# An expert network's first layer as 20 block products in place of 22, with the next group's first four products ahead of the token tiles

## The chip, the cores and the metric

One core of a Trainium2 chip. The metric is the device time of one launch in microseconds; three runs of the kernel before are shown, and one execution under the profiler.

## What is computed

Two blocks of a graph network with a feed-forward part, on 1250 nodes ("tokens") of 512 features. The change lies in the last part, the eight experts that every token passes, mixed by the leaf probabilities of a small decision tree:

```python
b, s, dim = x.shape                              # 1250 tokens, 512 features
leaf_probs = _leaf_probs(flat_x, rw, rb)         # [tokens, 8]
h = jnp.einsum('nd,edh->neh', flat_x, w1) + b1[None]     # first layer: 512 -> 2048 for each of 8 experts
h = jax.nn.gelu(h, approximate=False)
y = jnp.einsum('neh,ehd->ned', h, w2) + b2[None]         # second layer: 2048 -> 512
out = jnp.einsum('ned,ne->nd', y, leaf_probs)
```

The result is added to the running rows of the tokens. All else (the graph sums, the routing of the other expert layer) is left as it was.

## The kernel before

The changed part is `phase_tree`. The 8 x 2048 hidden columns are worked through in 64 **groups** of 256; two groups make a **pair** (the code's quarter `Q`), the first with even number `G`, the second with odd. Matrices in fp32 are multiplied in three passes (`cut_products`, lines 528 to 530): a rounded high part of each operand and the rest, high x high, high x low, low x high. So every operand has a "hi" (a ScalarE copy into the rounded type) and a "lo" (a VectorE subtraction).

First layer of a group: a 256 x 512 block of weights times 512 x 1250 tokens. The tokens stand in three blocks of 416, 416 and 418. The two of 416 are worked by Strassen's scheme, seven products of half blocks, of two 128-row slices each; the third directly, in eight slices. That is 7 x 2 + 8 = 22 block products of 128 x 128 x (416 or 418), 66 matmuls. The sums of weight blocks that Strassen's scheme wants are made by GpSimd (`weight_sums`, lines 1741 to 1746, four sums of 256 columns), their hi by ScalarE (L1785), their lo by VectorE (L2064). The sums of token blocks are made once, at the start (L1769, L2144, L2167 and around). Products are mixed by VectorE out of PSUM (L2079 to L2101, five a group); gelu with the bias on ScalarE, then hi (L1852) and lo (L2105).

Second layer of a pair: ten tiles of 125 tokens, each four slices of hidden columns x three passes, 120 matmuls of 512 columns (`second`); VectorE adds a tile into the token rows, weighted by the leaf probability (L2132). Eight tiles end in the pair itself, tiles 8 and 9 (`LATE`) inside the next pair's first group.

Every engine has its own queue, written out by hand as a loop over the groups, and works it strictly in order; engines wait for each other by counting semaphores. TensorE's queue holds in each group some products of the first layer, then "slots" with work of the second layer, then the rest. PSUM has eight banks: four for the token tiles, four for the first layer. Weights come by DMA from SyncE's queue into one buffer of 256 x 512 (`raw1`), from which GpSimd, ScalarE and VectorE read. The buffers of the weight sums are double, and the plain sums lie in the same place as their low parts.

Names of rows: `x_sums_hi`, `x_block_hi` are token operands, `w_sums`, `w_hi`, `w_lo` weights, `hidden` the gelu's in- and output.

Of the kernel before, what the change touches and what calls it, by code (L numbers as in the profile page):

```python
# [55 lines left out]
TBLOCKS = [(0, 416), (416, 832), (832, 1250)]  # L56
TBW = 416
# [1486 lines left out]
STEPS = 48  # L1544


def tree_buffers(nc, g, low, middle, high):
    room = Room(nc, low)
    g.xchi = room("x_sums_hi", [128, 7, 2, TBW], F32R)
    sums_at = room.next  # L1550
    g.xclo = room("x_sums_lo", [128, 7, 2, TBW], F32R)
    g.xcsum = Room(nc, sums_at)("x_sums", [128, 7, 2, TBW], F32)
    xf_at = room.next
    g.xf = room("f_xT", [128, KD, N], F32)
    node_at = room.next
    g.node_z = room("node_z", [7, N], F32)
    g.low_end = room.next
# [3 lines left out]
    g.b2b = Room(nc, node_at)("b2_by_token", [128, 2, D], F32)  # L1561
    assert over.next <= node_at and node_at + 2 * D * 4 <= g.low_end

    room = Room(nc, middle)
    g.p1 = room("first_product", [128, TBW], F32)
    g.u2 = room("second_sum", [128, TBW], F32)
    g.u3 = room("third_sum", [128, TBW], F32)
# [4 lines left out]
    g.x2hi = room("x_block2_hi", [128, KD, BW], F32R)  # L1572
    g.x2lo = room("x_block2_lo", [128, KD, BW], F32R)
    s1hi = room("w1_sums_hi1", [128, 4, 2, 128], F32R)
    sums_at = room.next
    s1lo = room("w1_sums_lo1", [128, 4, 2, 128], F32R)
    s1 = Room(nc, sums_at)("w1_sums1", [128, 4, 2, 128], F32)
# [5 lines left out]
    g.w1hi = room("w1_hi", [128, 2, KD, 256], F32R)  # L1583
    g.w1lo = room("w1_lo", [128, 2, KD, 256], F32R)
    s0hi = room("w1_sums_hi0", [128, 4, 2, 128], F32R)
    sums_at = room.next
    s0lo = room("w1_sums_lo0", [128, 4, 2, 128], F32R)
    s0 = Room(nc, sums_at)("w1_sums0", [128, 4, 2, 128], F32)
    g.shi, g.slo, g.ssum = (s0hi, s1hi), (s0lo, s1lo), (s0, s1)
    g.branch = room("branch", [TR, NT, 2, 7], F32)  # L1590
    g.pairs = room("branch_pairs", [TR, NT, 4], F32)
    g.leaf = room("leaf_by_token", [TR, NT, NE], F32)

# [5 lines left out]

def phase_tree(nc, sem, g, produce, rows):  # L1600
# [4 lines left out]
    w1hi, w1lo, w2hi, w2lo, raw1, raw2 = g.w1hi, g.w1lo, g.w2hi, g.w2lo, g.raw1, g.raw2  # L1605
# [6 lines left out]
    moved = sem("f_moved")  # L1612
    x_sum = sem("f_x_sum")
    x_sum_pool = sem("f_x_sum_pool")
# [9 lines left out]
    w1_hi = sem("t_w1hi")  # L1624
    w1_lo = sem("t_w1lo")
    s_sum = sem("t_s_sum")
    s_hi = sem("t_s_hi")
    s_lo = sem("t_s_lo")
# [3 lines left out]
    p1_moved = sem("t_p1_moved")  # L1632
# [12 lines left out]
    P1, P5, P6, P2, P7, P4, P3, D0, D1 = range(1, 10)  # L1645
    U2, U3, C22, C21, C12 = range(1, 6)
    ACTIVE_AT = {(0, 0): 1, (1, 1): 2, (0, 1): 3, (1, 0): 4, (2, 0): 5, (2, 1): 6}
    BANK_A, BANK_F, BANK_E, BANK_B = 4, 5, 6, 7
    X11, X21, X22, T1, T2, T3, T4 = range(7)
# [7 lines left out]
    def made(G, which):  # L1657
        return 9 * G + which

    def summed(G, which):  # L1660
        return 5 * G + which
# [5 lines left out]
    def block_count(Q, b, m):  # L1667

        return 6 * (2 * Q + m // 2) + ACTIVE_AT[b, m % 2]

    def tokens(of, b, m):
        return of[:, m, TBLOCKS[b][0]:TBLOCKS[b][1]]

# [7 lines left out]
    def wait_block_free(eng, Q, b):  # L1681
        if Q:
            eng.wait_ge(used, y_count(Q - 1, last_tile(b)))
# [8 lines left out]
    def x_block(i, j):  # L1692

        return g.xf[:, 2 * i:2 * i + 2, TBLOCKS[j][0]:TBLOCKS[j][1]]

    with nc.Block() as block:
        @block.sync
        def _(sp):
            def load1(n):
                e, p = divmod(n, 8)  # L1700
                if n:
                    sp.wait_ge(w1_lo, n)
                    sp.wait_ge(s_sum, 4 * n)
                sp.dma_start(raw1[:, :, :], w1_d[e, :, :, p * 256:(p + 1) * 256]).then_inc(w1_in, 16)
# [10 lines left out]
            for G in range(GROUPS):  # L1715
                if G + 2 < GROUPS:
                    load1(G + 2)
                if G + 1 < GROUPS:
                    load2(G + 1)
                if G % 8 == 0:  # L1720
                    e = G // 8
                    if e == 0:
                        sp.wait_ge(node_turned, 1)
                    elif e >= 2:
                        sp.wait_ge(b2_added, NT * (e - 1))
                    sp.dma_start(g.b2b[:, e % 2, :], g.b2[e:e + 1, :].partition_broadcast(128)).then_inc(b2_in, 16)
            for i in [0, 1, 2, 3, 4, 5, 7, 9]:
                store_out(sp, i)
# [3 lines left out]
        def _(q):  # L1732
            def weight_sums(n):

                a11, a12 = raw1[:, 0:2, 0:128], raw1[:, 2:4, 0:128]
                a21, a22 = raw1[:, 0:2, 128:256], raw1[:, 2:4, 128:256]
                s1, s2, s3, s4 = (g.ssum[n % 2][:, i] for i in range(4))
# [4 lines left out]
                q.tensor_tensor(s3, a11, a21, ALU.subtract).then_inc(s_sum, 1)  # L1742
                q.wait_ge(s_sum, 4 * n + 1)
                q.tensor_tensor(s2, s1, a11, ALU.subtract).then_inc(s_sum, 1)
                q.wait_ge(s_sum, 4 * n + 3)
                q.tensor_tensor(s4, a12, s2, ALU.subtract).then_inc(s_sum, 1)

            weight_sums(0)
            q.wait_ge(moved, 7)
            q.tensor_tensor(g.xcsum[:, T3], x_block(1, 1), x_block(0, 1),  # L1750
                            ALU.subtract).then_inc(x_sum_pool, 1)
# [15 lines left out]
        def _(a):  # L1767
            def hi_sum(which):
                a.activation(g.xchi[:, which], g.xcsum[:, which], ACT.Copy).then_inc(x_hi, 1)  # L1769

            def w1_high(n):
# [626 lines left out]
```

## Time and profile before

| | us |
|---|---|
| median of three runs | 2363.72 (2363.37 to 2366.75) |
| profiled execution | 2362.39, its span 2360.6 |
| TensorE busy in the span | 2232.0 (95%) |
| VectorE, ScalarE, GpSimd busy | 1358.8, 919.0, 408.6 |

The expert stretch begins near 650 us and lasts to the end. A row of the timeline has its start, its duration, engine, line, operation, what is written and read, and in brackets how long the engine stood idle before and who released it. Matmuls overlap in the rows, since their ends include the run through the array; pace is read from start to start. PEclk is the granted TensorE clock as a share of 2.4 GHz.

### The profile page before, as it was taken

Reading aid. Unit: us, or ns where it says so; the run is one execution under the profiler, and the core shown is the slowest. Engines: PE = TensorE matmul, PEld = TensorE weight load, DVE = VectorE, ACT = ScalarE, POOL = GpSimd, SP = SyncE. Lnnn points to the kernel's source line nnn. Section 1 sums busy time; section 2 is a strip of 40 time slices with the busy share of each in tenths; the row PEclk is TensorE's granted clock in tenths of the full one; section 3 lists DMA queues with packets and bytes.
Section 4 is the critical chain, followed back from the end, with each engine's and each line's share of the span. In section 5 each row is a group of like instructions: output and inputs, shape, how many; then the busy total and the mean of one; then the engine's idle time right before and its main releaser. Section 6 shows DMA issues by size and latency. Waiting matters only on the chain.

```text
span 2360.6 us, 31808 instructions
## 1 busy us (share of the span) xinstructions
PE 2232.0 (95%) x12255; PEld 1978.7 (84%) x12255; DVE 1358.8 (58%) x2143; ACT 919.0 (39%) x1474; POOL 408.6 (17%) x378
## 2 busy tenths in 40 slices
PE   3998998579999999999999999999999999999999
PEld 3887996449678888888888888888888888888887
DVE  7995356645465555555555555555555555555554
ACT  1335335245354344343334444443333443433332
POOL 1553000110121121121111121121111121121110
PEclk9999998689999999999999999999999999999999
DMA  2000202250011111111111111111111111111111
GB/s 69 2 2 1 72 1 81 83 162 14 27 41 36 45 43 43 45 44 42 36 37 42 44 45 42 43 45 36 36 41 45 36 50 45 36 45 41 36 36 53
DMA packets 70689, 101.92 MB, mean 43 GB/s; under 512 B 5519, under 2 KB 40927, under 8 KB 70543
## 3 DMA queue, kind: packets, MB, share of 16 engines
q1 hardware_dynamic: 67243, 94.20, 12.2%
q0 software_dynamic: 3040, 5.19, 0.8%
q8 instruction: 100, 1.64, 0.3%
q10 hardware_dynamic: 260, 0.51, 0.1%
q14 instruction: 46, 0.38, 0.1%
HBM read 92.14 MB, written 7.74 MB: 42 GB/s over the span
## 4 chain that ended last, share of the span: by engine, by line
PE 73%; DVE 1%; ACT 1%; issue 0%; DVEq 0%
PE psum L528 24%; PE psum L529 24%; PE psum L530 24%; DVE x_sums_lo L2144 0%; PE psum L1902 0%; ACT f_rows L522 0%; DVE stats L486 0%; DVE x_rows L2154 0%; PE psum L1892 0%; DVE norm_shift L495 0%; ACT x_sums_hi L1806 0%; PE psum L1909 0%; ACT L1836 0%; ACT dev L517 0%; DVE x_sums L2167 0%
## 5 line engine op out<-in xcount | busy, mean ns | idle before, releaser
L529 PE MATMUL psum<-w_lo,hidden_hi 128*125 128x512 f32 x1280 | 506.2, 395 | 0.0
L528 PE MATMUL psum<-w_hi,hidden_hi 128*125 128x512 f32 x1280 | 505.1, 395 | 0.0
L530 PE MATMUL psum<-w_hi,hidden_lo 128*125 128x512 f32 x1280 | 504.7, 394 | 0.0
L2132 DVE SCALAR_TENSOR_TENSOR x_rows<-psum,leaf_by_token,x_rows 125x512 f32<-125x512 f32 x320 | 232.5, 747 | 301.2 <-PE psum L530 301.2
L2105 DVE TENSOR_TENSOR hidden_lo<-hidden,hidden_hi 128x416 fp32r<-128x416 f32 (+1 forms) x384 | 258.9, 674 | 198.3 <-ACT hidden_hi L1852 198.2
L1741 POOL TENSOR_TENSOR w_sums<-w_raw 128x256 f32<-128x256 f32 x64 | 48.8, 762 | 1407.9 <-PE psum L530 1329.5
L530 PEld LDWEIGHTS psum<-w_hi,hidden_lo 128*125 128x125 f32 x1280 | 237.4, 185 | 60.7
L528 PEld LDWEIGHTS psum<-w_hi,hidden_hi 128*125 128x125 f32 x1280 | 237.9, 186 | 53.7
L529 PEld LDWEIGHTS psum<-w_lo,hidden_hi 128*125 128x125 f32 x1280 | 237.0, 185 | 53.0
L1841 ACT ACTIVATE hidden<-hidden,b1cols 128x416 f32<-128x416 f32 x192 | 122.8, 640 | 310.8 <-DVE hidden L2089 253.6
L1830 ACT ACTIVATE first_product<-psum 128x416 f32<-128x416 f32 x64 | 33.3, 520 | 516.5 <-PE psum L530 516.5
L1852 ACT ACTIVATE hidden_hi<-hidden 128x416 fp32r<-128x416 f32 (+1 forms) x384 | 212.5, 553 | 12.2
L528 PE MATMUL psum<-x_sums_hi,w_sums_hi 128*128 128x416 f32 x512 | 180.9, 353 | 1.1 <-DVE hidden L2089 1.1
L528 PE MATMUL psum<-x_block_hi,w_hi 128*128 128x418 f32 x512 | 180.6, 353 | 0.0
L530 PE MATMUL psum<-x_sums_hi,w_sums_lo 128*128 128x416 f32 x512 | 180.5, 353 | 0.0
L529 PE MATMUL psum<-x_block_lo,w_hi 128*128 128x418 f32 x512 | 180.1, 352 | 0.0
L529 PE MATMUL psum<-x_sums_lo,w_sums_hi 128*128 128x416 f32 x512 | 179.9, 351 | 0.0
L530 PE MATMUL psum<-x_block_hi,w_lo 128*128 128x418 f32 x512 | 179.5, 351 | 0.0
L528 PE MATMUL psum<-x_sums_hi,w_hi 128*128 128x416 f32 x384 | 135.5, 353 | 0.0
L529 PE MATMUL psum<-x_sums_lo,w_hi 128*128 128x416 f32 x384 | 135.1, 352 | 0.0
L530 PE MATMUL psum<-x_sums_hi,w_lo 128*128 128x416 f32 x384 | 135.1, 352 | 0.0
L2079 DVE TENSOR_TENSOR second_sum<-psum,first_product 128x416 f32<-128x416 f32 x64 | 37.8, 591 | 136.5 <-PE psum L530 136.5
(335 smaller groups left out, 3955.2 us busy)
## 6 DMA issues: line engine op xcount, KB each, us to landing
w_raw<-in_w SPq DMA_DIRECT2D x128, 512.0 KB, 3.4
expert_raw<-in_experts SPq DMA_DIRECT2D x8, 1024.0 KB, 5.7
expert_results_d<-expert_results SPq DMA_DIRECT2D x16, 160.0 KB, 4.6
x_rows<-in_x SPq DMA_DIRECT2D x1, 2500.0 KB
c_rows_d<-c_rows SPq DMA_DIRECT2D x10, 250.0 KB
W_raw<-in_gnn_W SPq DMA_DIRECT2D x4, 512.0 KB, 4.2
W_raw<-in_gnn_W SPq DMA_DIRECT2D x1, 2048.0 KB, 9.9
b_by_token<-in_b SPq DMA_DIRECT2D x8, 256.0 KB, 3.8
```

Source lines behind the costliest of these rows:

```text
L528: t.matmul(out, stat[0], mov[0], start=start, stop=False, skip_group_check=again)
L529: t.matmul(out, stat[0], mov[1], start=False, stop=False, skip_group_check=again)
L530: return t.matmul(out, stat[1], mov[0], start=False, stop=stop, skip_group_check=again)
L1741: q.tensor_tensor(s1, a21, a22, ALU.add).then_inc(s_sum, 1)
L1830: a.activation(g.p1[:, :], g.psum[:, BANK_A, 0:TBW], ACT.Copy).then_inc(p1_moved, 1)
L1841: a.activation(to, to, ACT.Gelu, bias=bias(G, j)).then_inc(active, 1)
L1852: a.activation(tokens(hhi, b, m), tokens(hid, b, m), ACT.Copy).then_inc(hi_cut, 1)
L2079: v.tensor_tensor(g.u2[:, :], bank(BANK_B), g.p1[:, :], ALU.add).then_inc(mixed, 1)
L2105: v.tensor_tensor(tokens(hlo, b, m), tokens(hid, b, m), tokens(hhi, b, m).bitcast(F32), ALU.subtract).then_inc(lo_cut, 1)
L2132: v.scalar_tensor_tensor(out=g.x_rows[:, i, :], in0=g.psum[0:TR, i % Y_BANKS, :], scalar=g.leaf[:, i, e:e + 1], in1=g.x_rows[:, i, :], op0 ...
```

## The change

The first layer of a group is now one scheme over two weight halves, four 128-row slices and three token blocks (418, 418, 414, padded to 418): 20 products of 128 x 128 x 418, 60 matmuls. Each product multiplies one linear form of token blocks (20 "forms", made once at the start by 27 VectorE operations, with hi on ScalarE and lo on VectorE) by one form of weight blocks (18 a group: 4 of them plain blocks, 14 sums, made by 15 GpSimd operations of 128 columns). Products are named D, B1, C1, A1, A2, E, B2, A3, B3, A4, F, B4, A5, B5, C2, A6 (four of these are two block products in a row). They accumulate in four banks, and between two products of a bank the value so far is read out: six ScalarE copies (P6, F9, P18, F2, F6, A4; F9 is the copy that goes to `v_part`) and eleven VectorE mixes (T12, T00, O00, T02, O02, T01, T11, V, O12, O01, O11) a group in place of one copy and five mixes. The products D, B1, C1, A1 of a group ("opened") stand right behind A6 of the group before; behind a second group that is ahead of the pair's remaining token tiles.

```diff
+    def weight_forms(room, n):
+        hi = room(f"w1_forms_hi{n}", [128, WFORMS, 128], F32R)
+        at = room.next
+        lo = room(f"w1_forms_lo{n}", [128, WFORMS, 128], F32R)
+        return hi, lo, Room(nc, at)(f"w1_forms{n}", [128, WFORMS, 128], F32)
...
+    PRODUCTS = counts("D B1 C1 A1 A2 E B2 A3 B3 A4 F B4 A5 B5 C2 A6")
...
                 q.wait_ge(w1_in, 16 * (n + 1))
                 if n >= 2:
-                    q.wait_ge(product, made(n - 2, P3))
-                q.tensor_tensor(s1, a21, a22, ALU.add).then_inc(s_sum, 1)
...
+                    q.wait_ge(product, made(n - 2, "A6"))
+                total(U3, raw(1, 0), ALU.subtract, raw(1, 1))
+                total(U1, raw(0, 1), ALU.subtract, raw(0, 2))
+                total(U2, raw(0, 2), ALU.subtract, raw(1, 2))
+                q.wait_ge(w_sum, w_summed(n, "U3"))
+                total(U4, raw(0, 1), ALU.add, u[:, U3, :])
...
+                q.wait_ge(w_sum, w_summed(n, "U12"))
+                total(U13, u[:, U12, :], ALU.subtract, raw(1, 0))
...
+            def w_high(n):
+                to = g.whi[n % 2]
                 a.wait_ge(w1_in, 16 * (n + 1))
                 if n >= 2:
-                    a.wait_ge(product, made(n - 2, D1))
+                    a.wait_ge(product, made(n - 2, "A6"))
+                a.activation(to[:, H0K0:H1K0 + 1, :].rearrange("p u c -> p (u c)"), raw1[:, 0, :],
+                             ACT.Copy).then_inc(w_hi, 1)
+                a.activation(to[:, H0K2:H0K3 + 1, :], raw1[:, 2:4, 0:128], ACT.Copy).then_inc(w_hi, 1)
+                a.wait_ge(w_sum, w_summed(n, "U13"))
+                a.activation(to[:, U1:U15 + 1, :], g.wsum[n % 2][:, U1:U15 + 1, :], ACT.Copy).then_inc(w_hi, 1)
...
             for G in range(GROUPS):
+                copy(G, "P6", "D", 0, 1, BX)
+                copy_v(G)
+                copy(G, "P18", "C1", 1, 1, BC)
...
+                if G + 1 < GROUPS:
+                    w_high(G + 1)
+                copy(G, "F2", "A2", 0, 0, B1)
+                if G % 2:
+                    high(G - 1, 1, 0)
+                    high(G - 1, 2, 1)
+                    gelu(G - 1, "O11", 1, 1)
+                    high(G - 1, 1, 1)
+                else:
+                    w2_high(G)
+                copy(G, "F6", "B2", 2, 0, B2)
...
+            def first_layer(G):
                 Q = G // 2
...
                 if G % 2:
+                    second(Q, 0, (0,))
+                    second(Q, 1, (0,))
+                    second(Q, 0, (1,))
+                    second(Q, 1, (1,))
                 elif Q:
+                    second(Q - 1, LATE, range(4))
+                t.wait_ge(mixed, summed(G, "T12"))
+                multiply(G, B1, 5).then_inc(product, 1)
+                if G % 2:
+                    second(Q, 2, (0, 1))
+                elif Q:
+                    second(Q - 1, LATE + 1, range(4))
+                t.wait_ge(copied, copies(G, "P6"))
+                multiply(G, BX, 10, True).then_inc(product, 1)
+                t.wait_ge(copied, copies(G, "F9"))
+                multiply(G, B2, 9).then_inc(product, 1)
+                t.wait_ge(copied, copies(G, "F2"))
+                multiply(G, B1, 13)
+                multiply(G, B1, 16).then_inc(product, 1)
+                t.wait_ge(copied, copies(G, "F6"))
+                multiply(G, B2, 0)
+                multiply(G, B2, 4).then_inc(product, 1)
+                t.wait_ge(mixed, summed(G, "T00"))
+                multiply(G, B1, 7).then_inc(product, 1)
+                t.wait_ge(mixed, summed(G, "O00"))
+                multiply(G, BX, 14, True).then_inc(product, 1)
+                t.wait_ge(mixed, summed(G, "T02"))
+                multiply(G, B2, 17).then_inc(product, 1)
+                t.wait_ge(copied, copies(G, "A4"))
+                multiply(G, B1, 1)
+                multiply(G, B1, 19).then_inc(product, 1)
...
+                if G % 2 or G == 0:
+                    first_layer_opened(G)
+                first_layer(G)
                 if G % 2:
+                    if G + 1 < GROUPS:
+                        first_layer_opened(G + 1)
+                    second(Q, 3, (0, 1))
                     for i in range(Y_BANKS):
                         second(Q, i, (2, 3))
...
                 if G % 2:
                     add_b2(Q)
+                    if G + 1 < GROUPS:
+                        w_rest(G + 1)
+                    low(G - 1, 1, 0)
+                    low(G - 1, 2, 1)
+                    low(G - 1, 1, 1)
+                else:
+                    w_rest(G + 1)
```

Line numbers of the changed kernel stand in the next rows. GpSimd's queue for one group, before: four sums, and the first of the next group (`w_raw` is the weight buffer; the number tells the two buffers of sums apart).

```order
L1741 TENSOR_TENSOR w_sums_10998<-w_raw 128x256 [waits t_product,t_w1_in]
L1742 TENSOR_TENSOR w_sums_10998<-w_raw 128x256
L1744 TENSOR_TENSOR w_sums_10998<-w_sums_10998,w_raw 128x256 [waits t_s_sum]
L1746 TENSOR_TENSOR w_sums_10998<-w_raw,w_sums_10998 128x256 [waits t_s_sum]
L1741 TENSOR_TENSOR w_sums_11005<-w_raw 128x256 [waits t_product,t_w1_in]
```

The same queue now, the first twelve of the fourteen rows of a group (one row is two sums):

```order
L1782 TENSOR_TENSOR w_forms_11000<-w_raw 128x128 [waits t_product,t_w1_in]
L1782 TENSOR_TENSOR w_forms_11000<-w_raw 128x128 x2
L1782 TENSOR_TENSOR w_forms_11000<-w_raw,w_forms_11000 128x128 [waits t_w_sum]
L1782 TENSOR_TENSOR w_forms_11000<-w_forms_11000,w_raw 128x128
L1782 TENSOR_TENSOR w_forms_11000<-w_raw,w_forms_11000 128x128
L1782 TENSOR_TENSOR w_forms_11000<-w_raw,w_forms_11000 128x128 [waits t_w_sum]
L1782 TENSOR_TENSOR w_forms_11000<-w_forms_11000,w_raw 128x128 [waits t_w_sum]
L1782 TENSOR_TENSOR w_forms_11000<-w_raw,w_forms_11000 128x128 [waits t_w_sum]
L1782 TENSOR_TENSOR w_forms_11000<-w_forms_11000 128x128 [waits t_w_sum]
L1782 TENSOR_TENSOR w_forms_11000<-w_raw,w_forms_11000 128x128 [waits t_w_sum]
L1782 TENSOR_TENSOR w_forms_11000<-w_forms_11000,w_raw 128x128 [waits t_w_sum]
L1782 TENSOR_TENSOR w_forms_11000<-w_forms_11000 128x128 [waits t_w_sum]
```

Four sums of 256 columns became fifteen of 128; the product that the first waits for is now the last of the group two before, not one with eight block products behind it.

ScalarE's queue at the beginning of a second group, before (`first_product` is the copy of a product, the next two rows round the next group's weights):

```order
L1830 ACTIVATE first_product<-psum 128x416 [waits t_mixed,t_product]
L1775 ACTIVATE w_hi<-w_raw 128x1024 [waits t_product,t_w1_in]
L1785 ACTIVATE w_sums_hi_11003<-w_sums_11005 128x1024 [waits t_s_sum]
L1836 ACTIVATE hidden<-psum,b1cols 128x416 [waits t_used,t_product]
L1852 ACTIVATE hidden_hi<-hidden 128x416 [waits t_active]
L1841 ACTIVATE hidden<-hidden,b1cols 128x416 [waits t_mixed]
```

And now, from the copy P6 to the copy F6: P6, F9, P18, three rows that round the next group's weights, F2, four rows of the first group's hidden columns, F6.

```order
L1895 ACTIVATE hidden<-psum 128x418 [waits t_used,t_product]
L1902 ACTIVATE v_part<-psum 128x418 [waits t_mixed,t_product]
L1895 ACTIVATE hidden<-psum 128x418 [waits t_used,t_product]
L1841 ACTIVATE w_forms_hi_10998<-w_raw 128x256 [waits t_product,t_w1_in]
L1843 ACTIVATE w_forms_hi_10998<-w_raw 128x256
L1845 ACTIVATE w_forms_hi_10998<-w_forms_11000 128x1792 [waits t_w_sum]
L1895 ACTIVATE hidden<-psum 128x418 [waits t_used,t_product]
L1917 ACTIVATE hidden_hi<-hidden 128x418 [waits t_active]
L1917 ACTIVATE hidden_hi<-hidden 128x414 [waits t_active]
L1907 ACTIVATE hidden<-hidden,b1cols 128x418 [waits t_mixed]
L1917 ACTIVATE hidden_hi<-hidden 128x418 [waits t_active]
L1895 ACTIVATE hidden<-psum 128x414 [waits t_used,t_product]
```

The rounding of the next weights (L1845, which waits for the last GpSimd sum) stands ahead of a copy, F2, that a product of the same group waits for; five rows further on is another such copy, F6.

## Rows read from the trace of the kernel before

**Rows 1.** The page, busy us and share of the span by engine.

```profile
PE 2232.0 (95%) x12255; PEld 1978.7 (84%) x12255; DVE 1358.8 (58%) x2143; ACT 919.0 (39%) x1474; POOL 408.6 (17%) x378
```

**Rows 2.** Windows: stretch, length, busy by engine (count), clock, DMA share, GB/s.

```profile
1000.00:1500.00 500.00, 500.00 (x2377) 443.43 (x2376) 279.42 (x384) 193.26 (x299) 85.90 (x76) 1.00 0.13 41
```

**Rows 3.** Timeline of TensorE, ends of three runs of matmuls in a pair.

```profile
1502.41 0.35 PE L528 MATMUL psum<-x_sums_hi,w_hi 128*128 128x416 f32 x1
...
1506.95 0.40 PE L528 MATMUL psum<-w_hi,hidden_hi 128*125 128x512 f32 x1
...
1509.76 0.35 PE L528 MATMUL psum<-x_sums_hi,w_sums_hi 128*128 128x416 f32 x1
```

**Rows 4.** Timeline of GpSimd at the start, two weight sums.

```profile
612.35 0.73 POOL L1744 TENSOR_TENSOR w_sums<-w_sums,w_raw 128x256 f32<-128x256 f32 x1
...
613.15 0.73 POOL L1746 TENSOR_TENSOR w_sums<-w_raw,w_sums 128x256 f32<-128x256 f32 x1
```

**Rows 5.** Groups of GpSimd by line: count, busy us, mean ns, idle before.

```profile
L1760 POOL TENSOR_TENSOR leaf_by_token<-branch_pairs,branch 125x80 f32<-125x80 f32 x1 | 0.4, 364 | 0.1
```

**Rows 6.** Timeline of VectorE and GpSimd side by side in a pair.

```profile
1516.16 0.59 DVE L2101 TENSOR_TENSOR hidden<-psum,second_sum 128x416 f32<-128x416 f32 x1 [0.17 <-PE psum L530]
1516.27 0.74 POOL L1741 TENSOR_TENSOR w_sums<-w_raw 128x256 f32<-128x256 f32 x1 [30.23 <-PE psum L530]
...
1516.67 1.43 DVE L2069 TENSOR_TENSOR w_lo<-w_raw,w_hi 128x1024 fp32r<-128x1024 f32 x1
...
1516.96 1.73 POOL L1742 TENSOR_TENSOR w_sums<-w_raw 128x256 f32<-128x256 f32 x1
...
1518.05 1.09 DVE L2105 TENSOR_TENSOR hidden_lo<-hidden,hidden_hi 128x416 fp32r<-128x416 f32 x1
```

**Rows 7.** The page, DMA issues of weights: count, KB each, us to landing.

```profile
w_raw<-in_w SPq DMA_DIRECT2D x128, 512.0 KB, 3.4
```

**Rows 8.** Timeline of VectorE: long low part, three bias additions, two mixes.

```profile
640.68 1.89 DVE L2144 TENSOR_TENSOR x_sums_lo<-f_xT,x_sums_hi 128x1664 fp32r<-128x1664 f32 x1 [1.60 <-ACT x_sums_hi L1806]
...
693.43 2.07 DVE L2121 SCALAR_TENSOR_TENSOR x_rows<-b_by_token,leaf_by_token,x_rows 125x512 f32<-125x512 f32 x3
...
1511.73 0.59 DVE L2089 TENSOR_TENSOR hidden<-psum,third_sum 128x416 f32<-128x416 f32 x1
1512.24 0.59 DVE L2095 TENSOR_TENSOR hidden<-third_sum,psum 128x416 f32<-128x416 f32 x1
```

**Rows 9.** Timeline of ScalarE: a long rounding, a copy, rounding and gelu.

```profile
639.07 1.58 ACT L1806 ACTIVATE x_sums_hi<-f_xT 128x1664 fp32r<-128x1664 f32 x1
...
1503.75 0.52 ACT L1830 ACTIVATE first_product<-psum 128x416 f32<-128x416 f32 x1 [16.66 <-PE psum L530]
...
1513.03 0.55 ACT L1852 ACTIVATE hidden_hi<-hidden 128x416 fp32r<-128x416 f32 x1
1513.49 0.63 ACT L1841 ACTIVATE hidden<-hidden,b1cols 128x416 f32<-128x416 f32 x1
1514.15 0.55 ACT L1852 ACTIVATE hidden_hi<-hidden 128x416 fp32r<-128x416 f32 x1
```

**Rows 10.** Timeline at the one wait of TensorE in the first group.

```profile
666.93 0.59 DVE L2089 TENSOR_TENSOR hidden<-psum,third_sum 128x416 f32<-128x416 f32 x1
...
667.58 0.46 PE L528 MATMUL psum<-x_sums_hi,w_sums_hi 128*128 128x416 f32 x1 [1.11 <-DVE hidden L2089]
667.87 0.35 PE L529 MATMUL psum<-x_sums_lo,w_sums_hi 128*128 128x416 f32 x1
```

**Rows 11.** Windows around a gap of TensorE at the start, as rows 2.

```profile
652.00:654.40 2.40, 0.00 (x0) 0.03 (x1) 2.40 (x4) 2.37 (x4) 0.82 (x1) 1.00 0.00 0
655.00:658.00 3.00, 3.00 (x8) 1.88 (x9) 3.00 (x5) 3.00 (x4) 0.00 (x0) 0.50 0.00 0
```

**Rows 12.** Timeline: the last tile turned, and the second group's first product.

```profile
652.38 0.58 ACT L1795 ACTIVATE f_xT<-psum 128x500 f32<-128x500 f32 x1
...
673.38 0.35 PE L528 MATMUL psum<-x_sums_hi,w_hi 128*128 128x416 f32 x1
```

More of the change, by code:

```diff
@@ L1582, in tree_buffers @@
     g.raw2 = room("w2_raw", [128, 2, D], F32)
[L1583 to L1589, printed above, removed]
+    even = weight_forms(room, 0)
+    g.whi, g.wlo, g.wsum = zip(even, odd)
     g.branch = room("branch", [TR, NT, 2, 7], F32)
@@ L1592, in tree_buffers, with counts @@
     g.leaf = room("leaf_by_token", [TR, NT, NE], F32)
+    g.node_z = room("node_z", [7, N], F32)
 def tree_sources(g):
     return g.w1.rearrange("e (k p) h -> e p k h", p=128), g.w2.rearrange("e (j p) d -> e p j d", p=128)
+def counts(names):
+    return {name: i + 1 for i, name in enumerate(names.split())}
 def phase_tree(nc, sem, g, produce, rows):
@@ L1838, in gelu_mixed, with copy, copy_v @@
-            def gelu_mixed(G, which, b, j):
-                to = tokens(hid, b, 2 * (G % 2) + j)
+            def copy(G, which, from_product, b, j, bank, scale=1.0):
+                a.wait_ge(product, made(G, from_product))
+                wait_block_free(a, G, b)
+                a.activation(slot_of(hid, G, b, j), g.psum[:, bank, 0:width(b)], ACT.Copy,
+                             scale=scale).then_inc(copied, 1)
+            def copy_v(G):
+                a.wait_ge(product, made(G, "B1"))
+                if G:
+                    a.wait_ge(mixed, summed(G - 1, "O11"))
+                a.activation(g.vpart[:, :], g.psum[:, B2, 0:TBW], ACT.Copy).then_inc(copied, 1)
@@ L1911, in node_turn @@
                 return ins
-            def half_product(bank, stat, which, start, stop):
-                for k in range(2):
-                    ins = cut_products(t, g.psum[:, bank, 0:TBW], (stat[0][:, k, :], stat[1][:, k, :]),
-                                       (g.xchi[:, which, k, :], g.xclo[:, which, k, :]), start and k == 0,
-                                       stop and k == 1, again=not start)
-                ins.then_inc(product, 1)
-            def weights(G, i, j):
-                c = slice(i * 128, (i + 1) * 128)
-                return w1hi[:, G % 2, 2 * j:2 * j + 2, c], w1lo[:, G % 2, 2 * j:2 * j + 2, c]
@@ L2097, in hidden_12, with bank @@
[L2097 to L2105 removed]
+            def bank(at, b):
+                return g.psum[:, at, 0:width(b)]
@@ new lines, in mix_o00, with mix_t02, mix_o02 @@
+            def mix_o00(G):
+                to = slot_of(hid, G, 2, 0)
+                v.wait_ge(mixed, summed(G, "T00"))
+                v.tensor_tensor(to, bank(BX, 2), to, ALU.add).then_inc(mixed, 1)
+            def mix_t02(G):
+                to = slot_of(hid, G, 0, 0)
+                v.wait_ge(product, made(G, "B3"))
+                v.wait_ge(copied, copies(G, "F2"))
+                v.tensor_tensor(to, bank(B2, 0), to, ALU.add).then_inc(mixed, 1)
+            def mix_o02(G):
+                to = slot_of(hid, G, 0, 0)
+                v.wait_ge(product, made(G, "F"))
+                v.wait_ge(mixed, summed(G, "T02"))
+                v.tensor_tensor(to, bank(BX, 0), to, ALU.add).then_inc(mixed, 1)
@@ L2180, in _ @@
[L2180 to L2208 removed]
+                if i == 5:
+                    w_rest(0)
```

605 lines of the change are left out of this document (319 added, 286 removed).

## The prediction

> **What bounds the kernel now.** I read the page's busy line first [rows 1], then busy time by stretch [rows 2], then the timeline of one pair of groups. TensorE is busy 95% of the span, and in the expert stretch 500.00 of 500 us at a granted clock of 1.00, while VectorE has 279, ScalarE 193 and GpSimd 86. So from about 670 us to the end TensorE is the bound: a matmul taken out shortens the span by its pace, and a wait put into TensorE's queue lengthens it by its length. The others have room on average, but what counts now is whether they are in time.
>
> The pace is read from start to start, since the durations overlap. From 1502.41 to 1506.95 stand 24 matmuls of 416 columns: 0.189 us each, so 0.190 for 418. From 1506.95 to 1509.76 stand 12 of 512: 0.234 [rows 3].
>
> **What it removes.** A group had 42 matmuls of 416 and 24 of 418 columns in the first layer: 42 x 0.189 + 24 x 0.190 = 12.50 us. Now it has 60 of 418: 11.40. That is 1.10 us per group, 69 us over the 63 groups after the first (the first stands in the start-up below). The second layer keeps its 120 matmuls a pair. This term is nearly sure.
>
> **What it adds: a wait in the second group of each pair.** The weight sums on GpSimd are overlaid with the low parts of the group two before, so they can't start until that group's last product, A6, is done. ScalarE rounds them (L1845, 1792 columns) ahead of the copy F2, and TensorE may not start A3 before F2. I count from the end of the issue of A6 of a first group. TensorE then has D, B1, C1, A1 (12 x 0.190 = 2.28), four token half-steps (12 x 0.234 = 2.81), A2 (0.57), two more (1.40), E and B2 (1.14): it is at A3 at 8.20 us. (In first groups 78 token-tile matmuls, 18.2 us, lie in between, so there the sums are hidden.) Will F2 be there?
>
> GpSimd: a 256-column sum alone takes 0.73 [rows 4] and an 80-column one 0.364 [rows 5]. By the line through both, 128 columns take 0.46. The next one can start 0.05 before the end (1516.27 + 0.74 against 1516.96 [rows 6]), or 0.07 after it when it needs its result (612.35 to 613.15 [rows 4]). Fifteen sums, two of them of the second kind: 13 x 0.42 + 2 x 0.53 = 6.5 us. The raw weights are there by then: they are asked for some 5 us before A6, and a load lands in 3.4 us [rows 7].
>
> But VectorE is at work at the same time. In [rows 6] the addition that reads PSUM (L2101, 0.59) runs beside a GpSimd sum (0.74) and neither is longer. The two that read SBUF twice take turns with GpSimd: the sum begun at 1516.96 ends at 1518.69, 0.59 after L2069 does, and the L2105 after it takes 1.09 in place of 0.59, ending 0.45 after that sum. So I add to GpSimd's 6.5 us what VectorE does from two SBUF inputs in that time: O11 and two low parts at 0.51 each, two or three bias additions at 0.69, two short weight rests at 0.36 [rows 8]: 1.5 + 1.7 + 0.7 = 3.9. GpSimd starts at 0.3 and ends at 10.7.
>
> For the bias additions no row shows whether they take turns too; their two inputs lie in SBUF as those of L2069 do, so I count them. "SBUF — State Buffer" of the Trainium skill, section "SBUF: two separate sides", says that the pair of ports is a lock held for a whole instruction, and that any VectorE instruction with two SBUF inputs takes it against GpSimd. By that rule they count. If they didn't, GpSimd would end at 9.0 and the sum below would be 53 us lower.
>
> ScalarE: 1664 columns take 1.58, so 1792 take 1.70; the following instruction starts 0.1 sooner, F2 at 12.35, and takes 0.52 [rows 9]: done at 12.87. TensorE after a wait: VectorE ended at 667.52, the matmul stands at 667.58, the one behind it 0.29 later in place of 0.19 [rows 10]: 0.16 in all. So A3 starts at 13.03, **4.8 us late**.
>
> Queued behind F2 on ScalarE in a second group are two roundings, a gelu and its rounding, then F6, for which B3 waits. Steps of 0.46 from one to the next, 0.66 from the gelu to its own rounding [rows 9]: F6 starts 0.46 x 4 + 0.66 = 2.50 after F2, at 14.85, ends at 15.37, and B3 can start at 15.53. A3's six matmuls end at 14.17: **1.4 us late**. On VectorE the long weight rest and three low parts are late too and T00 comes at about 16.3: 0.1. At the pair's end the second layer's weight rest is behind four mixes: 0.2. In all 6.5 us. In first groups the same walk shows margins of 0.1 to 0.2 us at A4, F and B4 and no wait.
>
> Bounds: had GpSimd no neighbour (end 6.8), F2 would end at 8.97, A3 would be 0.9 late and B3 1.4: 2.6 with the small ones. If every sum that names a wait steps at 0.53, GpSimd needs 1.3 more: 7.8. I take 6.5, since [rows 6] show turns. It happens in 31 second groups (the last has no weights to prepare): 202 us.
>
> **Clock.** After TensorE's 2.4 idle us at 652 the granted clock was 0.50, the lower level, from 655 to 658, as against 1.00 before [rows 11]. A wait of 4.8 us may bring that. Matmuls would take up to twice as long; A3 would then end at 15.3, still before B3 may start, so most is hidden. I take 0.4 us per pair (12 us), between 0 and 1.5 (the 3.0 us of that row at half pace with nothing hidden).
>
> **Start-up.** The last tile is turned at about 653 [rows 12]. Behind it VectorE now has 21 sums of 418 columns (about 0.56 each with waits, 11.8), ten low parts of 836 (0.95, by the 416- and 1664-column rows of [rows 8]; 9.5), logits (1.1), T12 (0.6) and the next weights' rests (3.9): T00 at about 681. Nine products (5.1) and a gelu table with it bring A6 to 688.5; the corresponding end before was 673.38 [rows 12]. That is +15 us, from 8 (if the low parts overlap better) to 25 (half clock, ScalarE late).
>
> **Sum.** The profiled execution took 2362.4 (span 2360.6), within 0.1% of the median, 2363.7. 2362.4 + 15 - 69 + 202 + 12 = **2522 us**, slower by 6.7%.
>
> **Rivals.**
> - GpSimd isn't held up: its share of 86 us in 500 speaks for it, the turns in [rows 6] against. Second groups wait 2.6 us: 2362 + 15 - 69 + 81 = 2389.
> - Faster. The weights come in time: it decides at F2. If GpSimd were through at 5.9 (fifteen sums in 5.6 us, 0.37 each), F2 would be done when TensorE asks, F6 too, and nothing but the start would be left: 2362 + 15 - 69 = 2308. For it: the rest of ScalarE's and VectorE's queues is in time by rows. Against: 0.37 is less than the line through [rows 4, 5] gives even alone. The break-even is a wait of 54 / 31 = 1.7 us per second group; F6's 1.4 is nearly that.
> - Slower still: the reaction chain T00, O00, F, T02, B4, A4's copy, A5 has margins of 0.1 to 0.2 us in both groups; if each handover costs 0.1 more than the rows, or the clock stays down into B3 to B5, a pair loses 1.5 us more: 2522 + 47 = 2569, and with the upper bounds of all terms 2606.
>
> **Chances.** The forecast 0.72 (its own range 2460 to 2570), slower still 0.12, GpSimd free 0.10, faster 0.05, a break-even 0.01. Range 2420 to 2585: it leaves out most of the free case, the fast one and the far end. A difference below 0.2% can't be told from none here. Faster by more than that 0.05, within it 0.03 (break-even and a part of the free case), slower 0.92.
>
> **What would show it.** In the profile of the changed kernel: GpSimd's sums (L1782) at a mean near 0.7 and not 0.46; ScalarE's L1845 waiting for GpSimd in every second group; TensorE idle in every pair, about 5 and 1.4 us, released by ScalarE's L1895; a pair lasting 57 to 58 us in place of 53; the granted clock below 1.00 in the expert stretch; the first group ending near 688. Wrong would be a TensorE that stays busy all through (then the time is near 2308), or idle time that VectorE releases in first groups as well.

## The result, and the profile after

| | us |
|---|---|
| median after | 2521.61 (2511.6 to 2525.28, four runs) |
| median before, on the same chip | 2365.23 (2363.37 to 2367.09, four runs) |
| ratio | 1.0654, 95% interval 1.0622 to 1.0687 |
| profiled execution after | 2525.28, its span 2523.4, mean granted clock 0.939 (before 0.980) |

The kernel became 6.5% slower; 2522 us was forecast. The page of the changed kernel, its busy line (which answers to [rows 1]) and the chain that ended last:

```profile
PE 2265.2 (90%) x11871; PEld 1968.7 (78%) x11871; DVE 1604.5 (64%) x2619; ACT 1059.1 (42%) x1862; POOL 612.1 (24%) x1081
...
PE 57%; POOL 11%; ACT 3%; issue 3%; DVE 1%; DMA 0%; POOLq 0%; ACTq 0%; SPq 0%; DVEq 0%
```

TensorE has 384 matmuls fewer, as intended (64 groups x 6), and yet is busy 33 us longer, over a longer span. GpSimd, an engine that is busy 24% of the time, holds 11% of the chain: 0.11 x 2523 = 278 us, or 9.0 us in each of 31 pairs, if all of it lies in their second groups (the sums of one take 9.15 us on average). The windows of the same kernel (columns as in [rows 2]): the stretch of [rows 2], and then four pieces of one pair.

```profile
1000.00:1500.00 500.00, 469.67 (x2101) 405.46 (x2101) 320.70 (x473) 215.64 (x381) 135.43 (x263) 0.95 0.13 40
...
1502.70:1505.80 3.10, 0.01 (x1) 0.00 (x0) 0.42 (x1) 2.15 (x3) 0.84 (x2) 1.00 0.00 0
1506.00:1508.00 2.00, 1.44 (x6) 0.85 (x5) 2.00 (x3) 1.97 (x5) 0.00 (x0) 0.70 0.03 8
1508.30:1513.50 5.20, 5.20 (x15) 4.96 (x16) 2.89 (x6) 2.48 (x5) 0.00 (x0) 0.50 0.01 2
1514.00:1520.00 6.00, 6.00 (x32) 5.82 (x32) 5.17 (x10) 3.29 (x7) 0.00 (x0) 1.00 0.00 1
```

TensorE now has 470 of 500 us in place of 500 of 500, and in each pair a stretch at the lower of its clock's two levels (1.2 GHz): in 5.2 us it gets through 15 matmuls, behind it through 32 in 6.0. The timeline of that pair, by engine (start, duration, and in brackets the idle time before and who ended it):

```profile
1494.18 0.35 PE L530 MATMUL psum<-x_forms_hi_late,w_forms_lo 128*128 128x418 f32 x1
1494.69 2.06 POOL L1782 TENSOR_TENSOR w_forms<-w_raw 128x128 f32<-128x128 f32 x3 [19.71 <-PE psum L530]
1497.86 1.92 DVE L2205 SCALAR_TENSOR_TENSOR x_rows<-b_by_token,leaf_by_token,x_rows 125x512 f32<-125x512 f32 x2
...
1502.36 0.35 PE L530 MATMUL psum<-x_forms_hi_first,w_forms_lo 128*128 128x418 f32 x1
1503.16 0.45 POOL L1782 TENSOR_TENSOR w_forms<-w_forms,w_raw 128x128 f32<-128x128 f32 x1
1503.65 1.70 ACT L1845 ACTIVATE w_forms_hi<-w_forms 128x1792 fp32r<-128x1792 f32 x1 [4.98 <-POOL w_forms L1782]
1505.25 0.50 ACT L1895 ACTIVATE hidden<-psum 128x418 f32<-128x418 f32 x1
1505.81 0.46 PE L528 MATMUL psum<-x_forms_hi_first,w_forms_hi 128*128 128x418 f32 x1 [3.10 <-ACT hidden L1895]
...
1507.66 0.50 ACT L1895 ACTIVATE hidden<-psum 128x414 f32<-128x414 f32 x1
1508.21 0.71 PE L528 MATMUL psum<-x_forms_hi_first,w_forms_hi 128*128 128x418 f32 x1 [0.77 <-ACT hidden L1895]
1508.72 0.55 PE L529 MATMUL psum<-x_forms_lo,w_forms_hi 128*128 128x418 f32 x1
...
1513.60 0.38 PE L528 MATMUL psum<-x_forms_hi_late,w_forms_hi 128*128 128x418 f32 x1
```

This is to be read down. A6's last matmul at 1494.18 lets GpSimd begin its sums after 19.71 idle us; the last ends at 1503.61. ScalarE has stood 4.98 us in front of L1845, rounds, and only then copies F2 (1505.25), that is A2's product, which has been done since 1500.2. TensorE, ready since 1502.55, begins A3 at 1505.81. Then F6 (1507.66) is late by what stands between it and F2, and B3 begins at 1508.21. From there matmuls are 0.35 us apart until 1513.60, not the 0.19 of [rows 3].

The waits between 800 and 2300 us (who waited, for whom: total us, times, longest):

```profile
POOL w_forms L1782 <- PE psum L530: 513.6, 26, 20.2
...
ACT w_forms_hi L1845 <- POOL w_forms L1782: 135.5, 26, 5.6
PEld psum L528 <- ACT hidden L1895: 120.3, 52, 4.0
...
PE psum L528 <- ACT hidden L1895: 97.6, 43, 3.7
```

26 pairs lie in this stretch: one long wait of GpSimd for A6, one of ScalarE for GpSimd and two of TensorE's weight loads ("PEld") for ScalarE per pair. TensorE waits in no first group. The pair shown is like the others: over all 31, A3 begins 3.2 to 3.85 us late, 3.5 on average, and a pair lasts 57.6 us from start to start, where it lasted 52.95.

### The profile page after: what moved, and what is told of

Its sections match the earlier page's. It is cut to its first block, busy times and chain, and to the rows that moved or that the text cites. A ratio compares the mean times of both kernels' runs of the same rounds, so it can differ in the third digit from the quotient of the medians.

```text
span 2523.4 us, 32827 instructions
## 1 busy us (share of the span) xinstructions
PE 2265.2 (90%) x11871; PEld 1968.7 (78%) x11871; DVE 1604.5 (64%) x2619; ACT 1059.1 (42%) x1862; POOL 612.1 (24%) x1081
## 4 chain that ended last, share of the span: by engine, by line
PE 57%; POOL 11%; ACT 3%; issue 3%; DVE 1%; DMA 0%; POOLq 0%; ACTq 0%; SPq 0%; DVEq 0%
PE psum L528 20%; PE psum L529 19%; PE psum L530 19%; POOL w_forms L1782 11%; ACT hidden L1895 1%; ACT hidden_hi L1917 1%; ACT hidden L1907 0%; DVE x_forms L2228 0%; DMA w_raw<-in_w 0%; ACT w_forms_hi L1845 0%; DVE x_parts L2228 0%; PE psum L1969 0%; DVE x_forms_lo L2239 0%; ACT x_forms_hi_late L1834 0%; DVE w_lo L2124 0%
## 5 line engine op out<-in xcount | busy, mean ns | idle before, releaser
L529 PE MATMUL psum<-x_forms_lo,w_forms_hi 128*128 128x418 f32 x1280 | 483.6, 378 | 0.0
L528 PE MATMUL psum<-x_forms_hi_first,w_forms_hi 128*128 128x418 f32 x640 | 249.2, 389 | 124.2 <-ACT hidden L1895 118.3
L529 PEld LDWEIGHTS psum<-x_forms_lo,w_forms_hi 128*128 128x128 f32 x1280 | 264.3, 206 | 10.2
L1907 ACT ACTIVATE hidden<-hidden,b1cols 128x418 f32<-128x418 f32 (+1 forms) x320 | 203.9, 637 | 114.3 <-DVE hidden L2144 92.0
L2189 DVE TENSOR_TENSOR hidden_lo<-hidden,hidden_hi 128x418 fp32r<-128x418 f32 (+1 forms) x384 | 229.6, 629 | 24.5 <-ACT hidden_hi L1917 24.5
L528 PE MATMUL psum<-x_forms_hi_late,w_forms_hi 128*128 128x418 f32 x640 | 243.8, 381 | 0.0
L530 PE MATMUL psum<-x_forms_hi_first,w_forms_lo 128*128 128x418 f32 x640 | 241.9, 378 | 0.0
L530 PE MATMUL psum<-x_forms_hi_late,w_forms_lo 128*128 128x418 f32 x640 | 240.0, 375 | 0.0
L1782 POOL TENSOR_TENSOR w_forms<-w_raw,w_forms 128x128 f32<-128x128 f32 x384 | 212.8, 561 | 5.0
L1917 ACT ACTIVATE hidden_hi<-hidden 128x418 fp32r<-128x418 f32 (+1 forms) x384 | 204.3, 548 | 7.1
L1845 ACT ACTIVATE w_forms_hi<-w_forms 128x1792 fp32r<-128x1792 f32 x64 | 108.3, 1692 | 162.2 <-POOL w_forms L1782 162.2
```

The source lines that it names most:

```text
L528: t.matmul(out, stat[0], mov[0], start=start, stop=False, skip_group_check=again)
L529: t.matmul(out, stat[0], mov[1], start=False, stop=False, skip_group_check=again)
L530: return t.matmul(out, stat[1], mov[0], start=False, stop=stop, skip_group_check=again)
L1782: q.tensor_tensor(u[:, to, :], a, b, op).then_inc(w_sum, 1)
L1845: a.activation(to[:, U1:U15 + 1, :], g.wsum[n % 2][:, U1:U15 + 1, :], ACT.Copy).then_inc(w_hi, 1)
L1907: a.activation(to, to, ACT.Gelu, bias=bias(G, j)).then_inc(active, 1)
```

## The experiments

The theory: GpSimd may not begin before A6, ScalarE works its queue in order, so F2 and F6 are late behind L1845, and TensorE with them; the half clock comes on top. The main rival: the finer chain of copies and mixes (six and eleven a group where there were one and five) is too slow by itself.

### The gate taken away: e1_sums_by_slot

Each sum waits only for the product that last read its slot, in an order that follows the products, and the load of the first layer's weights is asked for ahead of that of the second's.

```diff
-                if n >= 2:
-                    q.wait_ge(product, made(n - 2, "A6"))
+                free("A1")
                 total(U3, raw(1, 0), ALU.subtract, raw(1, 1))
...
+                free("B2")
                 total(U7, raw(0, 3), ALU.subtract, u[:, U3, :])
...
+                free("A6")
+                total(U5, u[:, U3, :], ALU.subtract, raw(1, 3))
...
+                if G + 2 < GROUPS:
+                    load1(G + 2)
                 if G + 1 < GROUPS:
                     load2(G + 1)
-                if G + 2 < GROUPS:
-                    load1(G + 2)
```

> GpSimd's sums of the group after next begin as soon as the product that last read their own slot is done (U3 after A1, U4 after A2, U7 after B2, U1 after B3, U2 after A5, U14 and U15 after B5; only U5 and the five behind it after A6), and the weights are loaded ahead of the second layer's. The same sums, the same products. Theory (GpSimd's sums hold ScalarE's queue, that holds F2 and F6, and TensorE's clock falls after the wait): after A6 GpSimd needs six dependent sums, 3.2 us, and some turns, so it ends near 5 us in place of 8.9; F2 is in time, B3 waits 0.7 us for F6, the clock stays at 1.00: 2333 us (2310 to 2350). Rival (the finer chain of copies and mixes costs the time, in both groups): not below 2480.

Measured: 2344.66 us, ratio to before 0.9916 (0.9887 to 0.9944), 177 us less than the change as made. Its window and its waits between 800 and 2300 us:

```profile
1000.00:1500.00 500.00, 495.88 (x2313) 428.23 (x2312) 363.56 (x527) 243.85 (x428) 172.09 (x291) 1.00 0.13 42
```

```profile
POOL w_forms L1782 <- PE psum L530: 163.8, 145, 2.3
...
PEld psum L528 <- DVE w_lo L2133: 17.8, 29, 0.8
...
PE psum L528 <- DVE hidden_lo L2198: 6.5, 25, 0.3
PE psum L528 <- DVE w_lo L2133: 3.9, 16, 0.4
```

GpSimd's waits for products have gone from 26 long ones to 145 short ones, TensorE's waits for ScalarE's copies (L1904 in this kernel) are gone, and the clock is at its upper level. The theory is borne out: the same products, copies and mixes in the same order run without the waits, so the rival that the chain itself is too slow falls. What is left of TensorE's waits is for VectorE. GpSimd's sums now begin 9.2 us before A6 ends and end 4.3 us after it. The finer waits, the order of the sums and the earlier load were not run apart: in the change the weights were asked for 5.6 us before A6 ended (1488.79 in the pair above), so sums that begin this early need the load as well.

### Only the queue turned round: e2_round_after_F6

GpSimd keeps its gate. In second groups ScalarE's L1845 stands behind F6, VectorE's long rest behind T01, and the rounding of the second layer's weights (L1854) later.

```diff
+                if G % 2 == 0 and G + 1 < GROUPS:
+                    w_high_sums(G + 1)
                 copy(G, "F2", "A2", 0, 0, B1)
...
                 copy(G, "F6", "B2", 2, 0, B2)
-                if G % 2:
-                    w2_high(G)
+                if G % 2 and G + 1 < GROUPS:
+                    w_high_sums(G + 1)
                 gelu(G, "O00", 2, 0)
```

> GpSimd as in the changed kernel; in second groups ScalarE's long rounding L1845 stands behind F6, the second layer's rounding behind the high part of O02, and VectorE's long rest behind T01. Theory (the place of L1845 in ScalarE's queue makes F2 and F6 late, and GpSimd's 8.9 us alone harm nobody): A3 and B3 don't wait, VectorE is late for A6 and C1 by 1 to 2 us a pair, the clock stays up: 2364 us (2335 to 2385). If GpSimd itself were the bound, or the finer chain: 2480 or more.

Measured: 2386.06 us, ratio 1.0091 (1.0061 to 1.012): 136 us less than the change, and 1 us outside what was expected. In one pair of its timeline GpSimd's first and last sum, the copy F2 between them, and then TensorE's matmuls that waited:

```profile
1432.04 2.06 POOL L1782 TENSOR_TENSOR w_forms<-w_raw 128x128 f32<-128x128 f32 x3 [19.94 <-PE psum L530]
...
1437.57 0.52 ACT L1900 ACTIVATE hidden<-psum 128x418 f32<-128x418 f32 x1 [1.55 <-PE psum L530]
...
1441.65 0.46 POOL L1782 TENSOR_TENSOR w_forms<-w_forms,w_raw 128x128 f32<-128x128 f32 x1
...
1444.82 0.46 PE L528 MATMUL psum<-x_forms_hi_late,w_forms_hi 128*128 128x418 f32 x1 [0.74 <-ACT hidden L1900]
...
1448.45 0.46 PE L528 MATMUL psum<-x_forms_hi_late,w_forms_hi 128*128 128x418 f32 x1 [0.50 <-DVE hidden L2181]
...
1450.59 0.46 PE L528 MATMUL psum<-x_forms_hi_first,w_forms_hi 128*128 128x418 f32 x1 [0.16 <-DVE hidden L2195]
```

GpSimd's sums take 10.07 us here, and over all pairs they end 10.5 us after A6, where they ended 9.5 after it in the change. F2 waits only for its own product, and A3 and B3 wait in no pair. So with GpSimd even later, three quarters of the loss against e1 (136 of 177 us) go when the copies aren't queued behind it: the position in the queues is the cause, ScalarE's for F2 and F6. VectorE's long rest, which waits for L1845, was moved with it and not apart. The long rounding now holds up the gelu and A4's copy (0.74 us), and VectorE's long rest a mix (0.50): I had counted less for these. It costs 41 us against e1.

### The turns of VectorE and GpSimd: e4_bias_late

The bias additions (L2205) go to the end of VectorE's second group.

```diff
-                    add_b2(Q)
                     if G + 1 < GROUPS:
                         w_rest(G + 1)
...
                     low(G, 1, 1)
+                    add_b2(Q)
```

> The two or three bias additions of a pair stand at the end of VectorE's second group, out of GpSimd's time. Theory as predicted (each takes turns with GpSimd's sums): GpSimd ends 1.1 to 1.7 us sooner, so does F2: 2525 - 31 x 1.4 = 2482 us (2465 to 2500). If they don't take turns, GpSimd ends as before, 2515 to 2530.

Measured: 2485.91 us, ratio 1.0513 (1.0408 to 1.0618); its two runs lie 21 us apart (mean clock 0.944 and 0.951), so the size is known badly. In the timeline of the profiled one GpSimd's first and last sum, and A3:

```profile
1428.52 2.06 POOL L1782 TENSOR_TENSOR w_forms<-w_raw 128x128 f32<-128x128 f32 x3 [20.11 <-PE psum L530]
...
1436.12 0.46 POOL L1782 TENSOR_TENSOR w_forms<-w_forms,w_raw 128x128 f32<-128x128 f32 x1
...
1438.77 0.46 PE L528 MATMUL psum<-x_forms_hi_first,w_forms_hi 128*128 128x418 f32 x1 [2.21 <-ACT hidden L1895]
```

The sums take 8.06 us from first to last in place of 8.92, and A3 waits 2.21 in place of 3.10: both 0.9 less. That pair of the change has two bias additions; the pair before it has three:

```profile
1436.26 2.06 POOL L1782 TENSOR_TENSOR w_forms<-w_raw 128x128 f32<-128x128 f32 x3 [19.86 <-PE psum L530]
...
1439.43 2.79 DVE L2205 SCALAR_TENSOR_TENSOR x_rows<-b_by_token,leaf_by_token,x_rows 125x512 f32<-125x512 f32 x3
...
1445.19 0.45 POOL L1782 TENSOR_TENSOR w_forms<-w_forms,w_raw 128x128 f32<-128x128 f32 x1
```

Its sums take 9.38. So with none, two and three additions beside them they take 8.06, 8.92 and 9.38 us: 0.43 to 0.46 an addition. The bias additions do take turns with GpSimd, as the rule of the Trainium skill that the prediction cites ("SBUF — State Buffer", section "SBUF: two separate sides") says; without a neighbour one takes 0.69 [rows 8], in the change two take 1.92. The prediction took from it that the lock is held for the whole instruction; measured here, an addition of 0.69 cost GpSimd less than that, 0.43 to 0.46.

### The clock by itself: e3_filler and e10_filler_full

Both leave the other engines' queues as they are and put matmuls whose results nobody reads ahead of TensorE's wait for F2, where it would idle: 22 of 92 columns in e3, 13 of 512 in e10 (into the one bank of the token tiles that is free then).

```diff
                 multiply(G, B2, 9).then_inc(product, 1)
+                if G % 2 and G + 1 < GROUPS:
+                    for _ in range(22):
+                        t.matmul(g.psum[:, BX, 420:512], g.whi[G % 2][:, U6, :], form_high(FORM_AT[9], FORM_AT[9] + 1)[:, 0, 0:92],
+                                 start=True, stop=True, skip_group_check=True)
                 t.wait_ge(copied, copies(G, "F2"))
```

> 22 idle matmuls of 92 columns into columns of a bank that nothing reads, ahead of A3 in second groups, where TensorE waits 3.4 us; all else as in the changed kernel. Theory (about a third of what a pair loses is the half clock that follows the wait): the clock stays at 1.00, the 15 matmuls behind B3 take 0.19 and not 0.35 each: 2.2 us a pair less, 2457 us (2440 to 2480). If the clock falls for another reason, or the slow matmuls cost nothing: 2520 or more.

Measured: 2508.16 us, ratio 1.0607 (1.0576 to 1.0638). That is a miss. The granted clock still falls in 28 of the 31 pairs; in the one shown A3 begins at half clock.

```profile
1438.89 2.55 PE L2054 MATMUL psum<-x_forms_hi_first,w_forms_hi 128*128 128x92 f32 x22
1442.61 0.72 PE L528 MATMUL psum<-x_forms_hi_first,w_forms_hi 128*128 128x418 f32 x1 [1.17 <-ACT hidden L1895]
1443.12 0.55 PE L529 MATMUL psum<-x_forms_lo,w_forms_hi 128*128 128x418 f32 x1
```

So e3 doesn't say what the clock costs, since it changed it little (mean 0.947 in place of 0.939). Hence the longer matmuls:

```diff
+                if G % 2 and G + 1 < GROUPS:
+                    if Q:
+                        t.wait_ge(y_added, y_count(Q - 1, 7))
+                    for _ in range(13):
+                        t.matmul(g.psum[0:TR, 3, :], hhi[:, 0, 0:TR], w2hi[:, 0, 0, :], start=True, stop=True, skip_group_check=True)
                 t.wait_ge(copied, copies(G, "F2"))
```

> 13 idle matmuls of 512 columns into the fourth token bank, free at that time, ahead of A3 in second groups: 3.0 us of work of the usual size where TensorE stood idle 3.4 us (the 22 of 92 columns took 2.4 us and left the clock as it was). Theory (the half clock is a price of the wait): the clock stays at 1.00 and a pair saves about 2.2 us: 2457 us (2435 to 2480). If it falls all the same, 2505 or more.

Measured: 2475.02 us, ratio 1.0466 (1.0445 to 1.0487).

```profile
1425.09 3.20 PE L2056 MATMUL psum<-w_hi,hidden_hi 128*125 128x512 f32 x13
1428.81 0.46 PE L528 MATMUL psum<-x_forms_hi_first,w_forms_hi 128*128 128x418 f32 x1 [0.53 <-ACT hidden L1895]
...
1431.21 0.46 PE L528 MATMUL psum<-x_forms_hi_first,w_forms_hi 128*128 128x418 f32 x1 [0.98 <-ACT hidden L1895]
1431.51 0.35 PE L529 MATMUL psum<-x_forms_lo,w_forms_hi 128*128 128x418 f32 x1
```

And the window behind B3's start, of the same run:

```profile
1431.20:1437.00 5.80, 5.79 (x29) 5.38 (x30) 5.23 (x11) 3.59 (x6) 0.00 (x0) 1.00 0.01 1
```

A3 and B3 still begin late (3.7 us after the last product's turn ends, 3.3 in the next pair, and then 1.1 us), but behind them matmuls are 0.19 us apart, and the clock falls in 2 of the 31 pairs. The mean clock is 0.975 in place of 0.939. The difference, 2521.6 - 2475.0 = 47 us or 1.5 us a pair (the change's own four runs spread over 14 us), is what the half clock costs on balance: A3 is as late as in the change, 3.5 us on average, and B3 0.4 us later. The rest of the loss, 2475 - 2345 = 130 us against e1, is the waits.

### The other part of the change undone: e5_not_ahead

The opened products stand behind the token tiles again.

```diff
-                if G % 2 or G == 0:
-                    first_layer_opened(G)
+                first_layer_opened(G)
                 first_layer(G)
                 if G % 2:
-                    if G + 1 < GROUPS:
-                        first_layer_opened(G + 1)
                     second(Q, 3, (0, 1))
```

> The other part of the change undone: a first group's D, B1, C1 and A1 stand at that group's beginning, behind the pair's token tiles, not ahead of them. Theory (they cover the time in which VectorE finishes the pair's low parts and the second layer's rest): the token tiles come 2.3 us sooner, before the rest of the second layer's weights is there, so TensorE waits 2 to 2.5 us more a pair: 2525 + 32 x 2.0 = 2589 us (2560 to 2610). Rival (the place doesn't matter, tiles cover themselves): 2515 to 2530.

Measured: 2623.56 us, ratio 1.1094 (1.1072 to 1.1117): 102 us more than the change, where I had expected 67; it lies outside the expected range.

```profile
1441.30 0.49 PE L528 MATMUL psum<-w_hi,hidden_hi 128*125 128x512 f32 x1 [2.18 <-DVE w_lo L2121]
...
1442.39 0.63 PE L529 MATMUL psum<-w_lo,hidden_hi 128*125 128x512 f32 x1
```

The second layer now catches VectorE's rest of its weights unfinished, 2.18 us in every pair, and in 19 of the 32 pairs, this one among them, the clock falls behind that wait (0.63 a matmul in place of 0.39). This part of the change helps: the four products cover that rest.

### What is left after the gate: e8_early_b2 and e9_early_w2

e8 is e1 with the bias additions late as in e4. e9 is e8 with the second layer's weights rounded, and their rest made, ahead of the next group's in second groups. Of e9 against e8:

```diff
+                if G % 2:
+                    w2_high(G)
                 if G + 1 < GROUPS:
                     w_high(G + 1)
                 copy(G, "F2", "A2", 0, 0, B1)
...
                 if G % 2:
+                    w2_rest(G)
                     if G + 1 < GROUPS:
                         w_rest(G + 1)
```

> The sums by slot and the bias additions at the end of VectorE's second group, both as before. GpSimd then ends another 1 us sooner; what TensorE still waits for (about 0.7 us a pair, for VectorE) shrinks little: 2335 us (2322 to 2346). If VectorE's part of the pair is what still binds, it moves up as the additions leave: at the low end.

Measured: 2349.06 us, ratio 0.9933 (0.9916 to 0.9949), no gain over e1 and above the expected range. GpSimd was expected to end another 1 us sooner, but its sums end 4.3 us after A6 in both runs, and no A3 or B3 waits for them. With GpSimd off the path its turns cost nothing, and the rest of the second layer's weights is still waited for ("PEld" is TensorE loading weights):

```profile
PEld psum L528 <- DVE w_lo L2133: 18.4, 29, 0.9
```

> As the run with both, and in second groups the second layer's weights are rounded and their rest made ahead of the next group's, not at the pair's end, where TensorE's token tiles wait 0.4 us for it. 2322 us (2308 to 2340). If the additional SBUF work in GpSimd's time costs as much as it saves: the same as the run before.

Measured: 2332.91 us, ratio **0.9861 (0.9844 to 0.9877)**, faster than both kernels. That wait is gone; what TensorE itself still waits for between 800 and 2300 us is 0.3 us a pair:

```profile
PE psum L528 <- DVE hidden_lo L2198: 6.7, 26, 0.3
```

So the 20 products with these rearrangements are worth 1.4% (a pair lasts 51.5 us, before 52.95), where the count of matmuls alone (2362 + 15 - 69) would have given 2308 us, 2.3%.

## Why the prediction was right

The time, the cause and the place were right; two terms were off in opposite directions, and that the sum came out so close is in part luck. The second group's first product, in TensorE's timeline after:

```profile
689.02 0.35 PE L528 MATMUL psum<-x_forms_hi_first,w_forms_hi 128*128 128x418 f32 x1
```

- **Start-up (+15).** 689.02 against 673.38 [rows 12]: +15.6, with the first group's end forecast at 688.5. The single items of VectorE's work in that sum were not tested apart. The clock was at its lower level from 663.7 to 670.5 and from 674.0 to 684.2, which the +15 did not have in it, only its upper bound of 25; T00 ended at 683.0 where about 681 was forecast. Whether this term fits for the reason given is open.
- **What follows it.** From there to the end of the span the change takes 2523.4 - 689.0 = 1834.4 us, before 2360.6 - 673.4 = 1687.2: +147, where -69 + 202 + 12 = +145 was forecast. If the -69 holds (the matmul count and the pace of 0.19 are as before), 216 us are lost, 7.0 a pair. The pairs of e9 bear the -69 out to some 4 us: 51.5 less the 0.6 that TensorE loses there is 50.9, 2.1 below the 52.95 before, where 2.2 was forecast.
- **GpSimd (0.3 to 10.7 after A6).** It begins 0.31 after the issue of A6 ends (1494.38) and ends at 9.2. The sums alone were counted at 6.5; the turns with VectorE cost 2.4, not 3.9. That they take turns is shown by e4; that each costs GpSimd the whole duration of its neighbour does not hold: two bias additions of 0.69 moved away in e4 gave GpSimd 0.86 back, not 1.38. The other neighbours were counted at 2.2 (1.5 and 0.7); the 8.06 of e4 leaves them about 1.5. The sign "a mean near 0.7" was off for the same reason: the page shows means of 0.56 and 0.59 us for two kinds of sum, over all groups.
- **A3 (4.8) and B3 (1.4).** From 1502.55, 0.19 after the start of the last matmul, to 1505.81 it is 3.26, and with the 0.11 that the second matmul loses 3.4; B3 by the same count 1.13. The step that was mis-sized is the turns: GpSimd ended 1.5 us sooner than forecast, and A3 was 1.4 sooner. The waits were 4.5 us in this pair, 4.4 on average, not 6.5.
- **Clock (0.4 a pair).** Also mis-sized, the other way. I had counted A3's matmuls alone as slow, and hidden behind F6. In this pair the clock fell under A3 (its fifth matmul) and stayed at the lower level past B3: 15 matmuls x 0.16 = 2.4 us in this pair. e10 gives 1.5 a pair on balance. Of the 31 pairs 8 have a stretch of 3.4 us and not of 6.8 (184 us together), in 9 the clock falls while TensorE still waits for F2, so that part of the stretch costs nothing, and where matmuls are faster B3 waits 0.4 us longer. "The clock stays down into B3 to B5" was in the rival "slower still", as a mechanism; it came true inside the forecast.
- **The rivals.** "GpSimd isn't held up" fell: it is held up, by 2.4 us of 8.9. "Faster" needed the copies in time; e1 and e9 show that it was the right picture of the kernel without the gate (2333 in e9 where 2308 was worked out; of the 25 us between, some 17 are the 0.55 us a pair that TensorE in e9 still loses around its wait for VectorE's low parts). Its condition, sums of 0.37 us, was not the way there. Nor was it enough by the prediction's own walk: F6 ends 2.50 + 0.52 us after F2's start, so with F2 just in time B3 would still have been 1.4 late. In e1 the sums end 4.3 us after A6, not 5.9, and neither A3 nor B3 waits.

Open: why the lower level lasts 3.4 us in one pair and 6.8 in another; and how the rest of the turns, about 1.5 us, falls on the VectorE instructions besides the bias additions.

## What to carry to other kernels

When work is added on a side engine, its busy share (24% here) says nothing: take the instruction that waits for it, list what is queued behind that one on the same in-order queue, and ask who waits for those. Let a buffer's reuse wait for the last reader of each slot, not of the whole set: that, with the sums in the products' order and the load asked for sooner, was worth 177 us here, and moving the waiting instruction behind the urgent copies 136 us. A wait of about 3 us on TensorE is to be counted with what the clock takes behind it (1.5 us a pair here), and an edit's parts tested apart: one part of this change cost, and the other, taken back, cost 102 us more.

## What the runs showed of the hardware that was not expected

- At each wait for F2 (3.10 us in the pair shown, up to 3.69) the granted clock fell to its lower level, in all 31 pairs, at the earliest 1.6 us before A3's start and at the latest 1.7 us behind it, and stayed there for 3.4 or 6.8 us. With 2.55 us of that wait filled by 22 matmuls of 92 columns it still fell in 28 pairs (2508 us, mean clock 0.947); with 13 matmuls of 512 columns in 3.20 us it fell in 2 (2475 us, 0.975). The two fillings differ in length and in kind of matmul, so which of the two counts isn't shown.
- VectorE beside GpSimd: three 128-column sums took 2.06 us at 1494.69 of the change, and 1.31 where each VectorE instruction beside them has one of its two inputs in PSUM, as in the timeline of e1:

```profile
1425.15 1.31 POOL L1782 TENSOR_TENSOR w_forms<-w_raw,w_forms 128x128 f32<-128x128 f32 x3
```

Two bias additions took 1.92 in place of 1.38. Both sides pay for the turns, and GpSimd pays less than the whole duration of its neighbour.
